# A token mixer in quarters of 256 positions, with x turned in 64x64 pieces on TensorE and part of the sum on GpSimd

## The reference, cut to what matters

```python
Wc = W[..., 0] + 1j * W[..., 1]                 # x: (64 c, 128 h, 64 n, 2)
dt_Lambda = dt[:, None, 0] * Lambda[None, :, 0] + 1j * (dt[:, None, 1] * Lambda[None, :, 1])
num = jnp.exp(dt_Lambda_neg) - 1
den = jnp.exp(dt_Lambda_neg * L) - 1            # L = 1024
Wc = Wc * num * _reciprocal(den * Lam, EPS)
P = dt_Lambda[..., None] * pos - P_max[..., None]
K = jnp.einsum('chn,hnl->chl', Wc, jnp.exp(P))  # (64, 128, 1024), real part
```

## Time and profile before

| what | us |
|---|---|
| median of 3 runs | 6468.88 (6466.54 to 6470.77) |
| the profiled execution: its own time | 6470.72 |
| its span, first to last instruction | 6469.0 |
| token mixer: first DVE instruction of the first step | 43.19 |
| token mixer: last copy out of PSUM ends | 446.4 |
| steps: start of the first to the last L407 (16 of them) | 48.3 to 422.7 |

### The profile page before, as it was taken

The page is one execution under the profiler, slowest core; times in us unless marked ns, Lnnn a source line. Parts: engine busy times, 40 slices in busy tenths (PEclk is TensorE's granted clock), DMA queues, the critical chain, the costliest instruction groups (busy, mean ns, idle before and its releaser), DMA issues. The chain is left out here.

```text
span 6469.0 us, 109402 instructions
## 1 busy us (share of the span) xinstructions
PE 5967.5 (92%) x33363; PEld 5445.7 (84%) x33363; DVE 5822.2 (90%) x4749; ACT 5225.1 (81%) x12983; POOL 5736.9 (89%) x3788
## 2 busy tenths in 40 slices
PE   4658689999999999999999999999999999999998
PEld 3433489999999999999999999999999999999997
DVE  7874599999999999999999999999999999999996
ACT  4536688888888888888888888888888888888885
POOL 2430599999999999999999999999999999999995
PEclk8769899999999999999999999999999999999999
DMA  2440121122221222221222212222212222112220
GB/s 56 97 94 0 63 76 70 68 77 85 85 74 64 79 80 84 85 72 66 74 85 85 79 61 77 79 85 84 74 64 79 79 85 84 67 66 79 85 79 32
DMA packets 96128, 478.57 MB, mean 74 GB/s; under 512 B 13089, under 2 KB 17329, under 8 KB 87410
## 3 DMA queue, kind: packets, MB, share of 16 engines
q1 hardware_dynamic: 95602, 471.63, 21.0%
HBM read 328.35 MB, written 143.24 MB: 73 GB/s over the span
## 5 line engine op out<-in xcount | busy, mean ns | idle before, releaser
L1079 POOL TENSOR_TENSOR s_ring<-s_bc,s_u_t 128x820 f32<-128x820 f32 x2048 | 3625.6, 1790 | 4.3 <-DMA s_bc<-rows_bc 4.3
L985 ACT ACTIVATE s_decay<-s_dt_t,a_neg 128x205 f32<-128x205 f32 x8192 | 3047.2, 420 | 428.9 <-DVE s_ring L1150 359.9
L882 PE MATMUL s_y_ps<-s_ring,ident 128*128 128x205 f32 x16384 | 3164.5, 343 | 142.8 <-POOL s_ring L1085 74.0
L882 PEld LDWEIGHTS s_y_ps<-s_ring,ident 128*128 128x128 f32 x16384 | 2888.4, 193 | 232.3 <-POOL s_ring L1085 139.1
L1144 DVE TENSOR_TENSOR_SCAN s_decay<-s_decay,s_ring 128x820 f32<-128x820 f32 x1216 | 2265.2, 1863 | 221.9 <-ACT s_decay L985 219.7
L1085 POOL TENSOR_TENSOR s_ring<-s_ring,s_bc 128x820 f32<-128x820 f32 x832 | 1607.3, 1932 | 55.4 <-DVE s_ring L1144 55.2
L1144 DVE TENSOR_TENSOR_SCAN s_ring<-s_decay,s_ring 128x820 f32<-128x820 f32 x832 | 1543.8, 1856 | 45.8 <-ACT s_decay L985 45.4
L915 PE MATMUL s_xch<-s_x_t,w_low 128*128 128x205 f32 x8192 | 1524.1, 338 | 0.5 <-ACT s_x_t L1025 0.2
L915 PEld LDWEIGHTS s_xch<-s_x_t,w_low 128*128 128x128 f32 x8192 | 1423.9, 190 | 32.7 <-issue 30.5
L1150 DVE TENSOR_TENSOR s_ring<-s_decay,s_bc 128x820 f32<-128x820 f32 x1216 | 1230.3, 1012 | 41.9
L307 POOL TENSOR_TENSOR t_mag<-t_mag,t_osc 128x512 f32<-128x512 f32 x128 | 167.1, 1342 | 273.0 <-ACT t_osc L293 273.0
(11 more groups left out here) (165 smaller groups left out, 4817.2 us busy)
## 6 DMA issues: line engine op xcount, KB each, us to landing
s_bc<-rows_bc SPq DMA_DIRECT2D x64, 3280.0 KB, 11.2
mixed<-t_res SPq DMA_DIRECT2D x32, 1024.0 KB, 10.0
s_x_in<-mixed SPq DMA_DIRECT2D x64, 512.0 KB
s_h<-mixed SPq DMA_DIRECT2D x64, 512.0 KB
before<-s_h SPq DMA_DIRECT2D x64, 512.0 KB
out<-s_h SPq DMA_DIRECT2D x64, 512.0 KB
s_x_in<-in_txt SPq DMA_DIRECT2D x64, 308.0 KB
s_h<-in_txt SPq DMA_DIRECT2D x64, 308.0 KB
```

What stands on the lines that cost most here:

```text
L882: last = nc.tensor.matmul(y_ps, ident[:, :], ring[:, c % RING, n * LEN:(n + 1) * LEN], start=False, stop=(c % 4 == 3 and n == CN - 1))
L985: last = A.activation(decay[s % 2][:, n * LEN:(n + 1) * LEN], dt_t[:, par, j, :], ACT.Exp, scale=t["a_neg"][:, j, n0 + n:n0 + n + 1])
L1079: nc.gpsimd.tensor_tensor(ring[:, s % RING, :].rearrange("p (n l) -> p n l", n=CN), bc[:, par, n0:n0 + CN, :], u_t[:, j, :].unsqueeze(1).b ...
```

## The change

The table is made for 256 positions and not 512 (`QL`), and four factors (NQ = 4) on the data give the four quarters. What belongs to it:

- Angles, rounding, difference, sine and magnitude are half as long per head.
- `xs` and its four copies are gone. PE reads `xg` itself with a step of two elements as the stationary operand, and turns it in pieces of 64 rows by 64 columns: 32 matmuls per step, which write `turned_x` (two banks, one for each side, that is four heads). `xg` now holds four heads on partitions 0 to 63 and four on 64 to 127, so a load of x is two DMAs.
- DVE multiplies straight into `gw` (with `gre`) and into `cross` (with `gim`), 1024 elements each, four instructions. The sum of the two is made by POOL, which multiplies the table in two halves of four heads and adds after each.
- A head's product is two matmuls of 256 positions, into the two halves of one bank. The first head's product of G-1 stands ahead of the turning of G on PE, the other seven behind it.
- ACT copies six of eight results out of PSUM and DVE two (the fourth and the eighth).
- A row of `res` goes to `mixed` in pieces of 256 positions (1 KB) and not 512 (2 KB); there are still two DMAs per group.
- The setup works on six places and not four (768 elements where it had 512, 512 where it had 128), in fewer instructions.

```diff
@@ token_mixer, semaphores and tiles @@
-        at = sb("t_at", [P, 4])
+        at = sb("t_at", [P, 2 + NQ])
-        gre = sb("t_gre", [P, 2, HEADS])
-        xg = sb("t_xg", [BATCH, 2, HG * 128])
-        xs = sb("t_xs", [BATCH, 2, 2, HG, 2, MODES])
+        gre = sb("t_gre", [P, HEADS, NQ])
+        xg = sb("t_xg", [P, 2, HG // 2 * 128])
+        cross = sb("t_cross", [P, HG, NQ, BATCH])
+        gw = sb("t_gw", [P, 2, HG, NQ, BATCH])
+        turned_x = ctx.enter_context(nc.psum_tensor("t_turned_x", [P, 2, 512], F32))
@@ SP @@
+            def load(G, half):
+                wait(sp, x_turned, G - 1)
+                for side in range(2):
+                    sp.dma_start(xg[64 * side:64 * side + 64, half, :]...
+                                 x[:, bass.ds(G * HG + HG // 2 * side, HG // 2), :]).then_inc(x_in[half], 16)
@@ ACT @@
-                for h in range(0, HG, 2):
+                for h in range(HG):
                     b = h % 4
-                    act.wait_ge(full[b], 2 * G + h // 4 + 1)
+                    if b not in DVE_BANKS:
+                        act.wait_ge(full[b], 2 * G + h // 4 + 1)
...
-                wait(act, table, HG * G)
+                wait(act, table, 2 * G)
@@ POOL @@
-                pool.wait_ge(sine_done, G + 1)
-                pool.wait_ge(mag_done, G + 1)
-                for h in range(HG):
-                    s = slice(h * HALF, (h + 1) * HALF)
+                for side in range(2):
+                    if side == 0:
+                        pool.wait_ge(sine_done, G + 1)
+                        pool.wait_ge(mag_done, G + 1)
                     nc.gpsimd.tensor_tensor(mag[:, half, s], mag[:, half, s], osc[:, s], ALU.mult).then_inc(table, 1)
+                    pool.wait_ge(crossed, 2 * G + side + 1)
+                    nc.gpsimd.tensor_tensor(flat(gw[:, half, heads, :, :]), flat(gw[:, half, heads, :, :]), flat(cross[:, heads, :, :]),
+                                            ALU.add).then_inc(scaled, 1)
@@ DVE @@
-                for order in range(2):
-                    for r in range(2):
-                        last = V.tensor_scalar(xs[:, half, order, :, r, :], src[:, :, :, r ^ order], 1.0, None, ALU.mult)
-                last.then_inc(swapped, 1)
...
+                dve.wait_ge(x_turned, G + 1)
                 wait(dve, full[3], 2 * (G - 1))
+                wait(dve, scaled, 2 * G)
+                for order, g, target in ((0, gre, gw[:, half, :, :, :]), (1, gim, cross[:, :, :, :])):
+                    for side in range(2):
+                        last = V.tensor_tensor(target[:, heads, :, :], data..., g..., ALU.mult)
+                        if order == 1:
+                            last.then_inc(crossed, 1)
@@ PE @@
+                pe.wait_ge(x_in[half], (G - half) * 16 + 32)
+                wait(pe, crossed, 2 * G)
+                if not first:
+                    products(G - 1, 1 - half, range(1))
+                for order in range(2):
+                    for h in range(HG // 2):
+                        for r in range(2):
+                            for side in range(2):
+                                src = xg[part, half, 128 * h:128 * h + 128].rearrange("c (n r) -> c r n", r=2)
+                                last = nc.tensor.matmul(
+                                    turned_x[64 * r:64 * r + 64, side, 256 * order + BATCH * h:256 * order + BATCH * h + BATCH],
+                                    src[:, r ^ order, :], ident[part, part], start=True, stop=True)
+                last.then_inc(x_turned, 1)
+                if not first:
+                    products(G - 1, 1 - half, range(1, HG))
```

More of the change, by code:

```diff
@@ L28 @@
 HALF = LK // 2
+NQ = 4
+QL = LK // NQ
+DVE_BANKS = (3,)
 EPS_TOK, EPS_LN = 1e-7, 1e-5
@@ L183, in token_mixer @@
         sgn = sb("t_sgn", [P, 1])
[L184 removed]
+        at = sb("t_at", [P, 2 + NQ])
         role = sb("t_role", [P, 2])
[L186 removed]
+        pos = sb("t_pos", [P, QL])
         rate = sb("t_rate", [P, HEADS])
@@ L433, in _, with products @@
             ident = t["ident"]
-            def products(G, half):
-                for h in range(HG):
+            def products(G, half, heads):
+                for h in heads:
                     b = h % 4
-                    if h == 0:
-                        pe.wait_ge(scaled, G + 1)
-                    pe.wait_ge(table, HG * G + h + 1)
+                    if b == 0:
+                        pe.wait_ge(scaled, 2 * G + h // 4 + 1)
+                        pe.wait_ge(table, 2 * G + h // 4 + 1)
@@ L441, in products @@
                     wait(pe, empty[b], 2 * G + h // 4)
-                    nc.tensor.matmul(kb[b][:, :], gw[:, half, h, :, :], mag[:, half, h * HALF:(h + 1) * HALF],
-                                     start=True, stop=True).then_inc(full[b], 1)
+                    for k in range(2):
+                        last = nc.tensor.matmul(kb[b][:, QL * k:QL * k + QL], gw[:, half, h, 2 * k:2 * k + 2, :],
+                                                mag[:, half, h * QL:(h + 1) * QL], start=True, stop=True)
@@ L445, in step @@
+                    last.then_inc(full[b], 1)
             def step(G, half, first):
-                pe.wait_ge(swapped, G + 1)
-                wait(pe, w_read, G)
-                for order, bank in ((0, wa), (1, wb)):
-                    for h in range(HG):
-                        last = nc.tensor.matmul(bank[:, h * BATCH:(h + 1) * BATCH],
-                                                xs[:, half, order, h, :, :].rearrange("c r n -> c (r n)"),
-                                                ident[0:BATCH, 0:BATCH], start=True, stop=True)
@@ L461, in weight_codes @@
+                last.then_inc(x_turned, 1)
+                if not first:
+                    products(G - 1, 1 - half, range(1, HG))
+            loop(pe, step, lambda G, half: products(G, half, range(HG)))
 def weight_codes(nc, dve, step, n, qw, part, word, wide, codes, planes):
```

140 lines of the change are left out of this document (60 added, 80 removed).

## The result

| | before | after |
|---|---|---|
| median of the runs, us | 6467.71 (6465.79 to 6470.77) | 6351.34 (6348.38 to 6355.26) |
| the profiled execution, us | 6470.72 | 6355.26 |
| its span | 6469.0 | 6353.5 |
| last copy of the mixer ends at | 446.4 | 330.0 |
| from there to the end of the span | 6022.6 | 6023.5 |

The changed kernel takes 0.9821 of the time before, 95% interval 0.9809 to 0.9833. All of it comes from the mixer, which ends 116.4 us earlier; what follows takes as long as it did.

The account below looks back on a forecast made before the run. VectorE, busy 89 of 100 us, was taken as the bound. With 17.3 us steps the mixer's last copy ends at 326.1 instead of 446.4: 6470.7 - 120.3 = 6350.4, said 6350; own range 6335 to 6385, full range 6310 to 6402.

Parts of the forecast that it names:

- The ring: Mixer step: sine, GpSimd's start and four instructions, seven angles, rounding and difference follow one another, 17.3 us a step.
- GpSimd's four: GpSimd's two multiplications and two sums of a mixer step, 1024 elements each, back to back: 9.6 us.
- angles behind its end: VectorE's angles left to run after GpSimd's last instruction in a mixer step: seven angles, 2.2 us.
- The stall: VectorE's angles in the mixer: a tensor_scalar meeting a GpSimd instruction lasts until that ends; one or two a step, about 2.4 us.
- Rival 1: VectorE's angles slip in beside GpSimd without waiting: step 13.9 us, time 6299; chance 10%.
- Rival 2: TensorE at half clock (20.5 us a step) or DMA packets (20.4) bound the mixer: time 6398; chance 18%.
- The other bound: DMA in a mixer step, if a packet costs the same whatever its size: 19.1 us, plus x.
- Rival 3: TensorE's turning at 0.213 us a record and half clock throughout: 27.3 us a step, time 6500, slower than before; chance 5%.
- first to second: Distance from the mixer's first rounding to its second, without copies out of PSUM but with three boundaries: 16.6 us.
- tail: From the mixer's last rounding start to its last copy's end: rounding, difference, sine, GpSimd, four heads' products, copy; 19.1 us.
- B: Follow-up theory: VectorE instructions with both operands in SBUF wait for GpSimd's instruction in progress; angles last up to 2.5 us.
- A: The prediction's mechanism: angles wait for GpSimd, whose last end sets the rounding; at first, only one-input instructions wait. Step 17.3 us.

Follow-up runs that it names:

- one product: Against the changed kernel, all eight heads' angles made by one tensor_tensor, quarter turn moved into rounding and the sine's bias: 6350.18 us, ratio to before 0.982.
- places in PSUM: Against the changed kernel, the positions (t_pos) are copied once into PSUM and the angles read them there: 6351.06 us, ratio to before 0.9814.
- one quadrant after another: Against the changed kernel, the 32 turning matmuls run quadrant by quadrant instead of changing quadrant with every matmul: 6353.68 us, ratio to before 0.9825.
- old copies: Against the changed kernel, x is again copied in two orders by four tensor_scalar and turned in 16 matmuls of 128 columns: 6407.55 us, ratio 0.9907.

## Why the prediction was right

**The ring.** The step was forecast at 17.3 us by one chain. From the step shown, 213.04 to 230.35:

| term | forecast | measured |
|---|---|---|
| GpSimd's four | 9.6 | 9.29 |
| angles behind its end | 2.2 | 2.44 |
| rounding, start to start | 1.25 | 1.27 |
| difference, to the sine | 2.3 | 2.32 |
| sine | 1.9 | 1.91 |
| start of GpSimd | 0.07 | 0.08 |
| together | 17.3 | 17.31 |

Two terms are off and cancel: an instruction of 1024 elements takes 2.35 us as said, but I added 0.18 from the earlier trace rows for each angle let by, and the longest sum is only 0.1 over the median (2451 ns for 2356); and there is 0.2 more behind GpSimd's end. That the sum comes out so exactly is also luck in another way. I had VectorE arrive 6.5 us after GpSimd's start, two angles held and six free behind them, and yet added up seven. It arrives at 7.1, one is held and seven follow. With two held the step is 17.0 us, as the run with the copies ahead of the sine shows. Roundings are 17.3 us apart in eight of the fifteen steps and 17.07 in the last three.

**The stall** was the step on which all stood, and the one that a reader who adds up VectorE's own 12.1 us would miss. The run with GpSimd's sum cut to 8 elements shows it by removal, the run with one product from both sides. "One or two angles a step of about 2.4 us" is what came: one of 2.2, or one of 2.46. The reading of its reach was too narrow: I spoke of tensor_scalars. The instructions with two operands in SBUF that were tried wait as well, as the two-input angles, the single product and the sum on VectorE show.

**Rival 1** (6299) has no place left: angles do wait, and where none does the step is still 17.0 (places in PSUM) or 15.3 (sum of 8 elements), not 13.9. Its chain was also short of VectorE's own angles, rounding and difference.

**Rival 2** (TensorE or DMA bound, 6398). TensorE is busy 60 us of 100 and pauses for 6.5 us in the step shown. Packets of 1 KB, from the queue's row of one step, 206.9 to 223.9 us:

```profile
q1 hardware_dynamic: 2197, 2.32, 57.2%
```

Twice the packets of the earlier trace rows take about the same share, 0.07 us each for 0.14. By bytes, 9 us a step, was right (57.2% of 17 us is 9.7). The other bound was added up too high: 2048 packets at 0.14 us over 16 engines are 18.0 us, not 19.1.

**Rival 3** (turning at 0.18 us a record or more): it is 1.19 / 64, 0.019. This is the term that I sized worst, 6.8 us for 1.19, since I took the distance from weight loads that follow one another. The rows do not give that half either: 137 ns for 190 is 0.72, which would have been 9.8 us. Besides, those 0.213 us a record were measured at granted clock 0.50, and the turning now runs at 1.00. It was hidden, and one quadrant after another shows that even 3.50 is. Here the trace agrees with the Trainium skill (TensorEngine Tiling (Array Packing), Key Properties) that tiles work in parallel: by that rule I had 1.7 us. Two changes of tiling a step stand in the 1.19 and the 0.3 us ahead of it; no run takes them apart.

**The terms beside.** Scaling 1.216 for 1.21 forecast; sine 1.91; copies 0.69; first rounding at 48.22 for 48.2; first to second 16.75 for 16.6; tail 19.4 for 19.1.

**What I missed: 3.6 us.** The last rounding starts at 310.6 and was forecast for 307.0. Three of the early steps take 18.65 us. ScalarE's timeline there:

```profile
68.61 1.28 ACT L293 ACT_TABLE_LOAD   x1 [10.28 <-DVE t_ang L407]
69.90 1.91 ACT L293 ACTIVATE t_osc<-t_ang 128x2048 f32<-128x2048 f32 x1
...
87.25 1.28 ACT L293 ACT_TABLE_LOAD   x1 [4.11 <-DVE t_ang L407]
```

The table load for the sine stands behind the wait for the difference in the steps written out ahead of the loop, and ahead of it in the loop's. So it adds 1.3 us to the ring there: 3 x 1.35 = 4.1 us, with 0.2 of the first step and less 0.7 of the last three. The kernel before has the same order in its first steps, and I read only steps of its loop.

The end of the mixer was forecast at 326.1 and came at 330.0; the profiled executions differ by 115.5 us, forecast 120.3. That the median of 6351.3 falls within 2 us of 6350 is in part luck, since the profiled execution lies 3.9 above it.

**What stays open.** A few microseconds can't be followed to the end. With places in PSUM the mixer ends 5.0 us earlier than in the changed kernel, and the time is the same; what follows the mixer took between 6018.2 us (old copies) and 6027.8 (places in PSUM) in the profiled executions, with no change there. The runs of one kernel lie up to 9 us apart (6345.23 to 6354.50 with places in PSUM), so gains of 3 to 5 us in the mixer can't be read from the times.

## What to carry to other kernels

Where VectorE and GpSimd both work from SBUF, ask of each VectorE instruction on the critical ring whether GpSimd will be busy when it starts; GpSimd's end, not VectorE's own sum, then sets the time, and starting 1.2 us earlier gained 0.2 us a step here. Making GpSimd's instructions fewer and longer made each such wait longer (1.49 us at most beside instructions of 1.27, 2.57 beside 2.35). Taking one operand from PSUM removed it at the price of a slower instruction, and paid only together with an earlier start. When costs are added up, follow the ring from one instruction to the same one a step later, with a line of it for each engine, and check whether the first steps outside the loop have the same order.

## What the runs showed of the hardware

- The wait is mutual and a whole instruction long: GpSimd's 2.35 us became 4.42 when a VectorE product of 2.28 was 0.08 us ahead of it.
- A tensor_scalar of 256 elements takes 402 ns from SBUF and 534 from PSUM; from PSUM its longest of 128 was 544 beside GpSimd, from SBUF 2572.
- An instruction of VectorE that takes one of its two operands from PSUM does not wait. In the scan stage 1216 multiply `s_decay`, a tensor in PSUM, by one in SBUF; they last 1010 to 1015 ns, although GpSimd is busy 90% of the span and 98% of the 1000 us from 2000. So this row is no exception to B, and the expectations that leaned on it for A read it wrongly; it is a second case beside the places in PSUM. The single line of the changed kernel:

```profile
L1154 DVE TENSOR_TENSOR s_ring<-s_decay,s_bc x1216: 1010/1012/1015, 619.0 to 6284.6; 128x820 f32<-128x820 f32 x174
```

- TensorE's granted clock from 200 to 300 us was 0.81, and 0.89 with one quadrant after another: more of the stretch was at the full 2.4 GHz and less at 1.2, and the time stayed the same. In the changed kernel the products behind the long wait run at half clock (0.50), the turning at full (1.00). The columns are those of the earlier trace rows:

```profile
196.00:200.00 4.00, 3.72 (x9) 3.04 (x10) 2.83 (x3) 1.71 (x4) 4.00 (x2) 0.50 0.43 123
...
203.00:204.30 1.30, 1.30 (x66) 1.12 (x65) 1.30 (x2) 1.29 (x3) 1.30 (x1) 1.00 0.00 0
```
